# Block transposes and transfers in place of TensorE's, jobs cut in halves, and a new place for each slot's jobs, in a kernel of attention between two half FFNs

## What is computed

```python
def _L0_attn_ref(x, Wq, Wk, Wv, Wo, bo):
    left = x[..., :E // 2]
    q = (left @ Wq.T).reshape(N, S, H, Dh)
    k = (left @ Wk.T).reshape(N, S, H, Dh)
    v = (left @ Wv.T).reshape(N, S, H, Dh)
    energy = jnp.einsum('nqhd,nkhd->nqkh', q, k)
    att = jax.nn.softmax(energy / scale, axis=2)
    out = jnp.einsum('nqkh,nkhd->nqhd', att, v)
    return out.reshape(N, S, E // 2) @ Wo.T + bo
def _L0_ffn_ref(x, w_freq_real, w_freq_imag, bias):
    x_freq = jnp.fft.fft(x, axis=-1)
    y_freq = jnp.einsum('bnd,do->bno', x_freq, w)
    return jnp.real(jnp.fft.ifft(y_freq, axis=-1)) + bias
x = x + 0.5 * _L0_ffn_ref(_layernorm(x), ...)
x = x + _L0_attn_ref(_layernorm(x), ...)
x = x + 0.5 * _L0_ffn_ref(_layernorm(x), ...)
```

## Time and profile before

| | us |
|---|---|
| median of 3 runs | 349.0 (346.52 to 349.45) |
| the profiled execution, its own time | 348.84 |
| its span, first to last instruction | 347.0 |
| busy: TensorE | 320.2 (92%) |
| busy: ScalarE | 252.1 (73%) |
| busy: VectorE | 176.8 (51%) |
| busy: GpSimd | 112.1 (32%) |

### The profile page before, as it was taken

The page is one execution under the profiler, slowest core; times in us unless marked ns, Lnnn a source line. Parts: engine busy times, 40 slices in busy tenths (PEclk is TensorE's granted clock), DMA queues, the critical chain, the costliest instruction groups (busy, mean ns, idle before and its releaser), DMA issues.

```text
span 347.0 us, 8720 instructions
## 1 busy us (share of the span) xinstructions
PE 320.2 (92%) x3453; PEld 122.9 (35%) x3457; DVE 176.8 (51%) x485; ACT 252.1 (73%) x266; POOL 112.1 (32%) x125
## 2 busy tenths in 40 slices
PE   8886898939999999999999999999999999898975
PEld 5543332312344333433343234433442333232323
DVE  1654346525666466646674666556464634352235
ACT  2100687845888888887888788888878898999831
POOL 5434252051291118411560147112611170015004
PEclk9999899978999999999999999999999999999999
DMA  7535245942941295109630684137301950000101
GB/s 212 200 140 177 57 114 185 155 152 86 245 127 62 90 243 160 31 35 270 140 108 33 221 176 122 36 128 156 112 32 72 165 163 31 33 2 3 53 9 62
DMA packets 19475, 39.90 MB, mean 115 GB/s; under 512 B 3680, under 2 KB 6112, under 8 KB 18528
## 3 DMA queue, kind: packets, MB, share of 16 engines
q1 hardware_dynamic: 18208, 38.04, 40.3%
q10 hardware_dynamic: 1216, 1.18, 1.4%
HBM read 26.63 MB, written 12.58 MB: 113 GB/s over the span
## 4 chain that ended last, share of the span: by engine, by line
PE 75%; DVE 14%; issue 4%; ACT 2%; POOL 2%; DMA 2%; ACTq 1%; DVEq 0%
PE ot L661 27%; PE misc L574 26%; PE scores L648 12%; PE misc L580 2%; ACT probs L533 2%; PE scores L549 2%; DVE kp L789 2%; PE misc L617 2%; DVE ot_t L858 1%; DVE kp L791 1%; DVE qp L789 1%; DVE qp L791 1%; PE scores L574 1%; PE scores L556 1%; DVE stats L762 1%
## 5 line engine op out<-in xcount | busy, mean ns | idle before, releaser
L533 ACT ACTIVATE probs<-scores 128x1024 f32<-128x1024 f32 x256 | 246.9, 1024 | 61.2 <-PE scores L648 59.6
L661 PE MATMUL ot<-probs,VS 128*32 128x512 f32 x1024 | 137.9, 603 | 4.4 <-ACT probs L533 2.6
L648 PE MATMUL scores<-QS,KS 32*128 32x512 f32 x512 | 65.3, 499 | 2.3 <-ACT probs L533 1.5
L648 PEld LDWEIGHTS scores<-QS,KS 32*128 32x128 f32 x512 | 24.8, 183 | 110.4 <-ACT probs L533 98.0
L661 PEld LDWEIGHTS ot<-probs,VS 128*32 128x32 f32 x1024 | 30.1, 110 | 33.4 <-issue 14.7
L426 POOL TENSOR_SCALAR veps<-mv 128x4 f32<-128x4 f32 (+1 forms) x25 | 5.7, 229 | 101.8 <-DVE mv L769 101.8
L574 PE MATMUL misc<-half_ffn,xT_in 128*32 128x256 f32 x464 | 31.7, 391 | 1.6 <-DVE half_ffn L992 1.3
L825 DVE SCALAR_TENSOR_TENSOR x_out<-misc,rstd,x_out 128x256 f32<-128x256 f32 x28 | 13.6, 484 | 34.5 <-PE misc L574 29.4
L574 PE MATMUL misc<-half_ffn,xT 128*32 128x256 f32 x448 | 30.0, 385 | 1.2 <-DVE kp L791 1.2
L437 POOL TENSOR_TENSOR sq_k<-kp 128x512 bf16<-128x512 f32 x8 | 8.3, 1040 | 63.7 <-DVE kp L789 63.7
L428 POOL TENSOR_TENSOR rstd<-veps,power 128x4 f32<-128x4 f32 (+1 forms) x25 | 25.3, 1011 | 2.1
(11 more groups left out here) (109 smaller groups left out, 273.2 us busy)
## 6 DMA issues: line engine op xcount, KB each, us to landing
KS<-k_scr SPq DMA_DIRECT2D x56, 128.0 KB, 5.4
QS<-q_scr SPq DMA_DIRECT2D x56, 128.0 KB, 2.9
x_in<-x SPq DMA_DIRECT2D x8, 512.0 KB, 4.7
xT_in<-x_t SPq DMA_DIRECT2D x8, 512.0 KB, 7.1
k_scr<-kp SPq DMA_DIRECT2D x8, 512.0 KB, 2.6
q_scr<-qp SPq DMA_DIRECT2D x7, 512.0 KB, 7.8
out<-x_out SPq DMA_DIRECT2D x14, 256.0 KB, 2.0
q_scr<-qp ACTq DMA_DIRECT2D x1, 512.0 KB, 3.3
```

The source lines that it names most:

```text
L533: nc.scalar.activation(probs[u % PRING][:, :, :], scores[u % SRING][:, :, :], ACT.Exp, scale=SCORE_SCALE).then_inc(exp_done, 1)
L648: last = mm(scores[(u + j // 2) % SRING][:, j % 2, :], KS[b % 2][rows, slot, kt * P:(kt + 1) * P].bitcast(F32R), QS[b % 2][rows, slot, :]. ...
L661: last = mm(ot[COL * j:COL * (j + 1), :], VS[b % 2][:, kt, h, :], probs[(u + j // 2) % PRING][:, j % 2, :], start=s % 8 == 0, stop=s % 8 == 7)
```

## The change

1. **Transposes.** The TensorE jobs `LT` (from batch 2 on) and `T3` are gone. VectorE transposes blocks of 32x32 from a strided view of `lh` or `x2` in SBUF (`turn_left`, one instruction of 512 elements per partition; `turn_x2`, two), SyncE stores the result to a new scratch tensor and loads it back rearranged, in pieces of 512 bytes, as `leftT` or `xT`. Features and tokens come in another order, which the weights and views follow.
2. **Halves.** `QT`, `KT`, `V` are cut by 256 columns, `WO` by tile, and some `F1` and `F2` by their two terms: `F1_0a` is the first term and needs no evacuation. They lie in a left and a right half of `misc`. The tables spread them over all slots.
3. **Place in a slot.** TensorE runs `value_quad(it, s)` ahead of the slot's jobs; VectorE runs `take_values` ahead of the slot's evacuations.
4. **Prologue.** The first FFN of batch 1 runs behind that of batch 0, into `scores0`, in place of 16 of 18 filler matmuls; VectorE evacuates it behind the first guard, and score quad 0 waits for that. The loads of the first K and Q rows are in two groups, not three, some issued by ScalarE.
5. **Orders of GpSimd and SyncE.** `rstd_of(1, 3)` comes ahead of `next_x(3)`; the transfers of item 1 are placed between the others.

```diff
-STEADY = {0: [("F1_0", 2)], 1: [("QT", 1)], 2: [("WO_0", -1)], 3: [("WO_1", -1)], 4: [("T3_0", -1)], 5: [("T3_1", -1)],
-          6: [("F1_1", 2)], 7: [("F1_2", 2)], 8: [("V", 1)], 9: [("F1_3", 2), ("N", 1)], 10: [("F2_0", -1), ("NT", 1)],
-          11: [("F2_1", -1)], 12: [("F2_2", -1)], 13: [("LT", 2)], 14: [("KT", 2)], 15: [("F2_3", -1)]}
+STEADY = {0: [("F1_0a", 2, LEFT)], 1: [("F1_0", 2, LEFT)], 2: [("WO_0", -1, LEFT), ("WO_1", -1, RIGHT)],
+          3: [("WO_2", -1, LEFT), ("WO_3", -1, RIGHT)], 4: [("F1_1a", 2, LEFT), ("F1_1", 2, LEFT)],
+          5: [("F1_2a", 2, LEFT), ("F1_2", 2, LEFT)], 6: [("F1_3a", 2, LEFT), ("F1_3", 2, LEFT)],
+          7: [("QT_0", 1, LEFT)], 8: [("QT_1", 1, LEFT), ("V_0", 1, RIGHT)],
+          9: [("V_1", 1, RIGHT), ("F2_0a", -1, LEFT)], 10: [("F2_0", -1, LEFT), ("N", 1, RIGHT)],
+          11: [("NT", 1, RIGHT), ("F2_1a", -1, LEFT)], 12: [("F2_1", -1, LEFT)],
+          13: [("F2_2a", -1, LEFT), ("F2_2", -1, LEFT)], 14: [("KT_0", 2, RIGHT), ("F2_3a", -1, LEFT)],
+          15: [("F2_3", -1, LEFT), ("KT_1", 2, RIGHT)]}
+BEGIN = {0: [("LT", 1, LEFT)], 1: [("KT_0", 1, LEFT)], 2: [("KT_1", 1, LEFT)],
+         3: [("QT_0", 1, LEFT), ("F1_0a", 2, RIGHT)], 4: [("F1_0", 2, RIGHT), ("QT_1", 1, LEFT)],
+         5: [("F1_1a", 2, LEFT), ("F1_1", 2, LEFT)], 6: [("F1_2a", 2, LEFT), ("F1_2", 2, LEFT)],
+         7: [("F1_3a", 2, LEFT), ("F1_3", 2, LEFT)], 8: [("V_0", 1, LEFT), ("N", 1, RIGHT)],
+         9: [("V_1", 1, LEFT), ("NT", 1, RIGHT)], 14: [("KT_0", 2, LEFT)], 15: [("KT_1", 2, LEFT)]}
...
-                if it + 3 < B:
-                    load_x(it + 3)
                 if it == 0:
                     k_out(1)
                 if it + 1 < B:
                     k_in(it + 1)
-                    q_in(it + 1)
+                if it >= 1:
+                    x2_through(it - 1)
+                    xT_in_from(it - 1)
+                if it + 3 < B:
+                    load_x(it + 3)
+                if it + 1 < B:
+                    q_out(it + 1)
+                if it + 2 < B:
+                    left_through(it + 2)
+                if it + 1 < B:
+                    q_in(it + 1, range(0, 2))
+                if it + 2 < B:
+                    leftT_in(it + 2)
+                if it + 1 < B:
+                    q_in(it + 1, range(2, LANES))
                 if it >= 1:
                     store_out(it - 1, 0)
...
             begin_x2(0)
             next_x(2)
-            rstd_of(1, 2)
             square(kp, sq_k, kp_step, 1)
             square(qp, sq_q, qp_step, 1)
+            rstd_of(1, 3)
             next_x(3)
-            rstd_of(1, 3)
             square(kp, sq_k, kp_step, 2)
             for it in range(1, B):
...
+                    value_quad(it, s)
                     run_jobs(it, s)
-                    value_quad(it, s)
...
+            def turn_left(b):
+
+                dve.wait_ge(normed, b + 1)
+                wait(dve, left_stored, 16 * (b - 2))
+                nc.vector.transpose(left_blocks[:, :, :, :].rearrange("p k t s -> p k (t s)"),
+                                    lh[:, :, :].rearrange("p t (f k) -> p k t f", k=HD // 32)).then_inc(left_turned, 1)
+
+            def turn_x2(b, i):
+                dve.wait_ge(evacuated, evac_count(f"WO_{2 * i + 1}", b))
+                wait(dve, x2_stored, 16 * b)
+                last = nc.vector.transpose(x2_blocks[:, :, 2 * i:2 * i + 2, :],
+                                           x2[:, 2 * i:2 * i + 2, :].rearrange("p t (f k) -> p k t f", k=E // 32))
+                if i:
+                    last.then_inc(x2_turned, 1)
+
...
-                        if s == 5:
-                            left_half(1)
-                        if s == 12:
-                            norm0_stats(3)
-                            norm_moments(0, 4)
-                        if s == 13:
+                        if s == 9:
                             left_half(2)
-                    else:
-                        if s == 5 and it + 3 < B:
-                            norm0_stats(it + 3, range(0, 2))
-                        if s == 6 and it + 3 < B:
-                            norm0_stats(it + 3, range(2, T))
-                            norm_moments(0, it + 4)
-                        if s == 11 and it + 2 < B:
-                            left_half(it + 2)
+                            turn_left(2)
+                    elif s == 8 and it + 2 < B:
+                        left_half(it + 2)
+                        turn_left(it + 2)
+                    if s == 11 and it + 3 < B:
+                        norm0_stats(it + 3, range(0, 2))
```

More of the change, by code:

```diff
@@ L94 @@
+ALL_JOBS = [(it, s, name, it + d, half) for it in range(PROLOGUE, EPILOGUE + 1)
+            for s, jobs in sorted(slots_of(it).items()) for name, d, half in jobs]
+HALF_OF = {(name, b): half for _, _, name, b, half in ALL_JOBS}
+ORDER = [(it, s, name, b) for it, s, name, b, _ in ALL_JOBS if name[-1] != "a"]
 INDEX = {(name, b): n for n, (_, _, name, b) in enumerate(ORDER)}
+LAST_EARLY = INDEX["NT", 0]
+LAST_AHEAD = INDEX["F1_3", 1]
+READY = [(name, b) for _, _, name, b, _ in ALL_JOBS if not LAST_EARLY < INDEX[name.rstrip("a"), b] <= LAST_AHEAD]
@@ L113, in quad_units, with evacuated_at, slot_of, count_of_slots_to @@
+def evacuated_at(it, s):
+    return [(name, b) for name, b in jobs_at(it, s) if name[-1] != "a"]
+def slot_of(name, b):
+    return next((it, s) for it, s, other, at, _ in ALL_JOBS if (other, at) == (name, b))
+def count_of_slots_to(it, s):
+    return len([1 for at, slot, _, _ in ORDER if (at, slot) <= (it, s)])
 def quad_units(s):
@@ L528, in _ @@
                 q_rows(act, 0, slice(0, 1), lane, first_rows_in)
+            for lane in range(2, LANES):
+                k_rows(act, 0, slice(1, SLOTS), lane, second_rows_in)
             for u in range(PAIRS * B):
@@ L578, in transpose_x2, with by_columns @@
                 for t in range(2):
                     for c in range(C):
-                        last = nc.tensor.transpose(bank[:, (C * t + c) * P:(C * t + c + 1) * P],
-                                                   x2[:, 2 * i + t, c * P:(c + 1) * P], ident[:, :])
-                return last
+                        last = nc.tensor.transpose(into[:, c, :, t, :], x2[:, 2 * i + t, c::C], ident[:, :])
+                return last
+            def by_columns(dst, terms, parts=None):
+                for c in range(len(terms)) if parts is None else parts:
+                    weights, rhs = terms[c]
+                    for j in range(P // COL):
+                        last = mm(dst[COL * j:COL * (j + 1), :], weights(j), rhs, start=c == 0, stop=c == len(terms) - 1)
+                return last
@@ L600, in job @@
+                parts = None
+                if name[0] == "F" and (name.rstrip("a") + "a", b) in HALF_OF:
+                    parts = [0] if name[-1] == "a" else [1]
+                kind, i = name[:2], int(name.rstrip("a")[-1]) if "_" in name else 0
+                if kind == "F1":
                     pe.wait_ge(xt_loaded[b % 2], 16 * (b // 2 + 1))
-                    last = by_columns(bank[:, 0:E], [(xT_in[b % 2][:, c, i * P:(i + 1) * P], half_ffn[:, c, :])
-                                                     for c in range(C)])
+                    last = by_columns(half, [(columns_of(xT_in[b % 2][:, c, :], i * P), half_ffn[:, c, :])
+                                             for c in range(C)], parts)
@@ L709, in _ @@
             pe.wait_ge(ffn_summed, 2)
-            spectral(scores[0][:, 0], are_t, cos_var_sb)
+            spectral(scores[0][:, 0], are_t, cos_var_sb, C)
             pe.wait_ge(ffn_summed, 4)
-            spectral(scores[0][:, 1], aim_t, sin_sb)
+            spectral(scores[0][:, 1], aim_t, sin_sb, C)
             pe.wait_ge(ffn_summed, 6)
-            for t in range(T):
-                job(f"F1_{t}", 0)
-            keep_awake(18)
+            for b in range(2):
+                for t in range(T):
+                    job(f"F1_{t}", b)
+            keep_awake(2)
             pe.wait_ge(ident_loaded, 16)
@@ L1010, in _ @@
             guard(0)
-            norm0_stats(1)
-            norm_moments(0, 2)
+            for s in range(T + 6, 2 * T + 6):
+                run_jobs(PROLOGUE, s)
+            left_half(1)
             for it in range(B):
                 for s in range(QUADS):
-                    run_jobs(it, s)
                     if s == 7:
```

302 lines of the change are left out of this document (179 added, 123 removed).

## The result

| | before | after | forecast |
|---|---|---|---|
| median of the runs, us | 348.54 (346.52 to 349.45, 14 runs) | 349.85 (from 348.77, 14 runs) | 337 |
| ratio to before | | 1.0042, 95% interval 1.0022 to 1.0062 | 0.966 |
| profiled execution; its span | 348.84; 347.0 | 348.77; 347.0 | 337.1; 335.3 |

What follows compares the result with a forecast made beforehand. TensorE was taken to set the pace of full slots. Iteration 0 -6.5, iterations 1 to 5 -3.1, iterations 6 and 7 -2.2, tail +0.1 sum to -11.7 from 348.84: 337 us, range 332 to 341 (chance 0.45).

Steps and rivals of the forecast that it cites:

- Iteration 0 (-6.5): First iteration: VectorE's 5.24 us idle wait for GpSimd's rstd goes, taking it from 46.5 to 40.0 us.
- Work of a steady iteration (34.4): TensorE's work per steady iteration without the three transposes: 22.6 + 11.6 + 0.3 = 34.4 us, halves at 0.445 each.
- an operation of 512 elements is 0.69: VectorE's queue in steady iterations: duration used to sum waits, with each new transpose at 0.72 us.
- rival A: VectorE's strided transposes are slow, 1.25 us each if elements take twice as long: 345.6 us; chance 0.13.
- With values ahead of jobs there is a new limit ... Only slots 0 and 1 are such a pair, about 0.1: Steady iterations: two slots need 3.5 us plus one job; 3.94 against 3.70 of work for two halves, costing about 0.1.
- 3.5 plus one job: Minimum time in us of two slots together when value quads go ahead of jobs, set by exponentials.
- Waits on VectorE in slots 0, 9 and 10: Steady iterations: TensorE waits 0.2 us in slot 0, 0.2 for job 9, 0.8 for job 10.
- Slot 8's 0.34 for 0.4: Steady iterations: value quad 8 waits 0.4 us, the values' transpose standing behind F1_3 and its statistics and moments.
- Transfers (cost 0): Stores and reloads of xT and the left half, and Q rows, land in time; margin 0.2 us, cost 0.
- Rival B: Q rows come late as transfers hinder each other, up to 365 us; chance 0.08 slower, 0.07 about even (348).
- Prologue (0): Start of the kernel: batch 1's F1 replaces filler matmuls and its evacuations replace statistics, at no cost.
- the term that I bounded at 3: Prologue: VectorE's evacuations and statistics for batch 1's F1, costing at most 3 us if their cover is gone.

Runs made afterwards that it cites:

- e3: Kernel before, with only GpSimd's rstd_of(1, 3) put ahead of next_x(3) in iteration 0: 347.76 us, ratio 1.0004.
- e2: Changed kernel with VectorE transposes reading runs of 32 elements, weight rows permuted to match, xT loaded in four transfers: 347.82 us, ratio 0.9995.
- e1: Changed kernel with jobs ahead of the value quad again on TensorE, and evacuations ahead of take_values on VectorE: 339.48 us, ratio 0.974.
- e7: Kernel before, with only the value quad put ahead of jobs and take_values ahead of evacuations: 351.36 us, ratio 1.0067.
- e6: e1 with the two x2 transposes spread over two slots instead of together in one: 337.1 us, ratio 0.967.
- e12: e10 with SyncE's store of batch 1's q ahead of the loads of x in iteration 0: 335.66 us, ratio 0.960.
- e11: e10 with, in iterations 1 to 5, left half behind V_1's copy, half the Q loads ahead of the left store, reload last: 353.49 us, ratio 1.0128.
- e8: e6 with the first K and Q rows loaded in three groups, all issued by SyncE: 340.96 us, ratio 0.978.
- e9: Changed kernel with TensorE's jobs ahead of the value quad in slot 11 alone, where NT is: 352.56 us, ratio 1.0119.
- e5: Changed kernel with TensorE's jobs ahead of the value quad in slot 12 alone, the guard's slot: 350.78 us, ratio 1.0051.
- e10: e6 with batch 1's eight Q loads ahead of SyncE's wait for the left transpose in iteration 0: 340.2 us, ratio 0.9735.

## Why the prediction was wrong

- **Iteration 0 (-6.5): right,** -5.9. The Q rows let the score quad start 37.3 into it (36.6 in my sum), and the last slot takes 3.29 with its low clock (1.85 + 1.5). KT_0's wait for `leftT`, 1.6, lies inside the wait for the Q rows and wasn't named. The reason was half right: alone, GpSimd's order gives at most 1.6 of it (e3).
- **Work of a steady iteration (34.4): right,** to 0.1. Halves cost halves.
- **"an operation of 512 elements is 0.69", applied to the new transposes: the first step that failed.** That is rival A's first half, at a factor of 1.6 (1118 and 1172 for 707). Rival A's way of pricing, with the measured durations, gives +0.8 in slot 5 and +0.45 in slot 10; it was +0.54 and +0.24, so half to two thirds of a longer transpose shows. Against the forecast that is some 0.8 per iteration, 4 in all; e2, which takes the stride away, wins 0.7 to 1.1. The Trainium skill, "SBUF — State Buffer", section "Specifications (TRN2)", speaks of cachelines of 16 bytes and a price for each crossing; the direction agrees with e2, the factor here is 1.6. I gave this rival 0.13, on the ground that copies write in pieces at the plain rate, a row of another operation that strides in writing, not in reading.
- **"With values ahead of jobs there is a new limit ... Only slots 0 and 1 are such a pair, about 0.1": the step that failed most.** e1 prices the place at 8.8 in the spans, the guard's part (next point) and 1.4 of low clock in iteration 0 included. I looked for pairs of short slots and didn't apply my own 3.5 plus one job to a short slot followed by a full one. In a steady iteration half a job and then a full one are at least 3.5 + 0.89 = 4.4 for 4.15 of work: slots 1 and 2 take 4.41, slots 7 and 8 take 4.51, and the row of slot 8 names the exponentials. With an empty slot ahead it is 4.4 for the 4.1 of my sum. Iterations 6 and 7 have these; slot 2 of iteration 6 takes 2.70 for 2.30, slot 7 2.27 for 1.87. Together with the guard's 0.5 and a wait of 0.63 for `xT` in slot 9 that is why iteration 6 lost 1.1 and didn't win it, and e7 shows the place's part in the old kernel, +1.6.
- **The guard's branch was not in the sum at all.** Whatever a job feeds outside of the jobs has a slot's 0.97 less when jobs go behind values. The flag's chain (NT, copy, four small operations, 1.17 to TensorE) had 0.3 to spare in e1 and lacks 0.4 to 0.6 in the changed kernel. In six iterations at 0.57 that is 3.4.
- **Waits on VectorE in slots 0, 9 and 10: right** to 0.3 in each. Slot 8's 0.34 for 0.4 is luck: I had it wait for the values' transpose, which is done at 172.15, and the value quad starts at 172.50, behind exponentials; in e1 the wait is gone.
- **Transfers (cost 0): right in steady iterations of this kernel,** and by a thin margin, as said; in iteration 6 `xT` came 0.63 late. Rival B didn't decide here, but e2, e6 and e12 ran into it in single iterations and e11 in all five, in the wait for `leftT` more than in that for the Q rows that I had named. e1 didn't, in iterations 1 to 5.
- **Prologue (0): wrong by about 1,** and not by the term that I bounded at 3: the evacuations of batch 1's F1 end 2.8 ahead of the first score quad. I had put no price on the two groups of loads, which delay the first Q rows by 0.8 to 1.2 (e8).

The median of e6 is 337.1, my forecast. That is luck: it gets there without the new place and by another sum, 35.94 per iteration without transfer waits for 36.4, a prologue of 37.33 for 36.27, and 40.64 in iteration 0 for 40.0.

Which half of the place matters, TensorE's or VectorE's, was not separated: e1 and e7 move both. The waits that changed are for exponentials and the flag, which TensorE's half would explain; e9 moves it alone, in one slot, and the wait for the flag goes.

## What to carry to other kernels

When work is moved behind a consumer in an in-order queue, list everything that waits for that work's results outside the queue's own rhythm (a flag, a branch, another engine's next step), and test the limit on every order of empty, half and full slots, not only on the steady pattern. Price an operation with a new access pattern by a row that has that pattern in the same direction, and if there is none, let the slow case weigh in the forecast. Once engines keep pace, transfers with two landings in a row (store and reload) are next: issue them in the order in which they are needed, and keep bulk loads behind them.

## What the runs showed of the hardware

- VectorE's 32x32 transpose of 128x512 f32 reads a source with a stride of 4 or 8 elements in 1172 and 1118 ns, runs of 32 elements in 711 and 683.
- From the end of the instruction that writes the flag to the first matmul behind TensorE's load of it and branch: about 1.17 us (1.07 to 1.22 where it waited: after, e2, e5).
- A store of 512 KB took 2.6 us (k's median before). q's in iteration 0, issued right behind loads of 2 MB (K and x), took 7.8 to 10.3 in the kernel after and its versions, and 7.2 behind the 1 MB of K alone, with x issued after it (e12).
- TensorE fell to the lower of its two levels (granted clock 0.50) behind waits of 1.6 and 1.3 in a row (kernel after), 1.8 (e2) and 4.8 us (e10, a value quad of 1.96 for 1.07), and not behind waits of 2.0 (e12, 1.07), 2.5 (e1) and 2.8 (e11, iteration 3). The length of the last wait alone doesn't tell it.
